# An orthogonal convolution by per-frequency solves: half 1's stores beside forming, the tables' products beside half 1's transform, two copies on ScalarE

## What is computed

```python
xfft = rfft2(pad(gn(x), 1), norm='ortho')            # 34 x 18 frequencies, 128 x 32 each
vfft = transpose(rfft2(weight, s=(34, 34)))          # 128 x 127 per frequency
vH   = conj(swapaxes(vfft, -1, -2))
wfft = vH @ vfft
wfft = wfft + eps[..., None, None] * eye(127)        # eps: mean diagonal * 1e-5
W    = I - 2.0 * (vfft @ solve(wfft, vH))            # 128 x 128 per frequency
z    = irfft2(W @ xfft)[..., 1:-1, 1:-1] + bias
out  = x + z
```

## Time and profile before

| | us |
|---|---|
| profiled execution | 3139.8 |
| its span, first to last instruction | 3137.1 |
| TensorE busy | 2606.8 (83%) |
| VectorE busy | 2014.0 (64%) |
| ScalarE busy | 1269.0 (40%) |
| GpSimd busy | 742.2 (24%) |
| mean granted clock of TensorE | 0.869 |

### The profile page before, as it was taken

How to read it: one execution, slowest core, us unless ns; L and a number is a source line. 1 busy time by engine, 2 the same in 40 slices (tenths; PEclk the granted TensorE clock), 3 DMA queues, 4 the chain that set the end, 5 groups by cost and what they waited for, 6 DMA issues and landing times. The chain is left out here.

```text
span 3137.1 us, 89161 instructions
## 1 busy us (share of the span) xinstructions
PE 2606.8 (83%) x38281; PEld 2133.8 (68%) x38281; DVE 2014.0 (64%) x3842; ACT 1269.0 (40%) x2963; POOL 742.2 (24%) x1307
## 2 busy tenths in 40 slices
PE   3994919889999888998886968778888879959999
PEld 3663915555666677877775747566676768859999
DVE  5453710779788787787778889697887782003333
ACT  0441402443534255555533534343454444632221
POOL 0340000312121042332431414031343242520000
PEclk7897969989999899999988989797988899976787
DMA  4348073314231064754733516060231232566662
GB/s 171 104 110 149 2 121 67 123 56 163 68 113 40 15 129 81 139 110 80 158 67 62 109 29 135 3 136 13 93 95 53 65 120 77 164 140 162 169 168 92
DMA packets 562599, 310.00 MB, mean 99 GB/s; under 512 B 484616, under 2 KB 495496, under 8 KB 561368
## 3 DMA queue, kind: packets, MB, share of 16 engines
q1 hardware_dynamic: 520896, 183.58, 28.5%
q0 software_dynamic: 41312, 120.73, 11.4%
HBM read 162.85 MB, written 141.30 MB: 97 GB/s over the span
## 5 line engine op out<-in xcount | busy, mean ns | idle before, releaser
L1386 DVE SCALAR_TENSOR_TENSOR arena<-arena,psum 128x512 f32<-128x512 f32 (+2 forms) x608 | 399.0, 719 | 280.2 <-PE psum L1016 279.9
L1349 DVE TENSOR_TENSOR arena<-arena 128x960 f32<-128x960 f32 (+24 forms) x480 | 420.2, 876 | 16.6
L1344 DVE TENSOR_TENSOR arena<-arena 128x960 f32<-128x960 f32 (+8 forms) x600 | 403.9, 723 | 8.3
L953 PE MATMUL psum<-arena 128*32 128x256 f32 (+1 forms) x2904 | 263.9, 430 | 90.9 <-DMA arena<-plain 73.9
L995 PEld LDWEIGHTS psum<-arena 32*32 32x32 f32 x9280 | 160.5, 118 | 256.9 <-issue 240.4
L871 POOL COPY arena<-arena 128x512 f32<-128x512 f32 (+2 forms) x160 | 87.1, 594 | 1040.0 <-ACT arena L1159 1040.0
L1016 PE MATMUL psum<-arena 32*128 32x64 f32 x9280 | 313.1, 282 | 9.8 <-ACT arena L1180 9.8
L1016 PEld LDWEIGHTS psum<-arena 32*128 32x128 f32 x9280 | 291.7, 197 | 34.5 <-ACT arena L1180 20.4
L995 PE MATMUL psum<-arena 32*32 32x64 f32 x9280 | 187.0, 235 | 135.9 <-DVEq L1378 125.7
L957 PE MATMUL psum<-arena 128*32 128x256 f32 (+1 forms) x3696 | 264.5, 373 | 0.0
L1159 ACT COPY arena<-arena 32x128 f32<-32x128 f32 (+3 forms) x496 | 222.2, 448 | 31.4 <-DVE arena L1386 12.5
(11 more groups left out here) (121 smaller groups left out, 4764.9 us busy)
## 6 DMA issues: line engine op xcount, KB each, us to landing
blocks<-arena POOLq DMA_DIRECT2D x145, 256.0 KB, 2.5
arena<-blocks SPq DMA_DIRECT2D x290, 128.0 KB, 2.8
kept<-arena POOLq DMA_DIRECT2D x145, 256.0 KB, 3.0
arena<-kept SPq DMA_DIRECT2D x145, 256.0 KB, 2.8
xhat<-arena SPq DMA_DIRECT2D x32, 580.0 KB, 13.0
arena<-xhat SPq DMA_DIRECT2D x580, 32.0 KB, 2.6
yhat<-arena POOLq DMA_DIRECT2D x290, 64.0 KB, 2.3
arena<-x SPq DMA_DIRECT2D x8, 2048.0 KB, 11.7
```

What stands on the lines that cost most here:

```text
L953: pe.matmul(columns[quadrant(p)].rearrange("p (a k) n -> p a k n", k=m), K["ident"][:, quadrant(p)], spread(base[:, 0:m, :], 1, n), start= ...
L1344: ins = dve.tensor_tensor(pr, spread(R[:, t, :, :, j], 3, 2 * w_), both, ALU.mult)
L1349: link(dve.tensor_tensor(rest, rest, pr[:, :, h], op))
L1386: ins = dve.scalar_tensor_tensor(old, old, K["mask"][:, piv:piv + 1], upd_bank(u, c)[:, 0:L * n].rearrange("p (t n) -> p t n", n=L), ALU.m ...
```

## The change

- `statistics` of half 0 moves in front of VectorE's wait for the correlations in stage one. The two instructions that form `eps_all` move to stage two, behind the normalization of the second sample.
- The 48 term products, their copies and with them their stores go between the parts of half 1 instead of half 0. SyncE loads row blocks 0 and 1 at the start of stage two as before, and blocks 2 to 7 behind the 16 stores of half 0; its loads of half 1's x have no row loads between them any more.
- The 16 stores of half 1 leave stage two. SyncE issues them in the solver, behind the first two table loads of form a. The first users of the memory that `xs` shares wait for them: `load_tables` of the first pre job, ScalarE's first copy to `staged`, VectorE's first `place`. For this, group a's part of `M` and group b's change places (`HOME`), and `ce`, the factors, moves below `M`.
- `copy_p` and `copy_q` move from GpSimd to ScalarE. In mid, ScalarE does `copy_p(m + 1)` right behind `copy_j(m + 1)`; in final, `copy_q(m)` right behind `copy_jq(m)`. GpSimd keeps the stores and the resets. ScalarE now waits at the start of a mid and of a final job for the updates of the sweeps before.

```diff
@@ -35,7 +35,7 @@
 SLOTS_OF = [FIRST[n + 1] - FIRST[n] for n in range(5)]
 GROUPS = [(0, 1, 2), (3, 4)]
 NT = max(len(sets) for sets in GROUPS)
-HOME = [0, 82]
+HOME = [NQ - 82, 0]
 RESIDENT = NQ
 NTERM = 5
 UNITS_OF_SET = [[8] * 4, [8] * 4, [6] * 3, [8] * 4, [8, 8, 8, 7]]
...
@@ -259,7 +259,14 @@
         mv = forward(HALF, 2)
         FORWARD_TOP = forward.at
         s_x = [ctx.enter_context(nc.semaphore(f"s_x{i}")) for i in range(4)]
-        s_mv = ctx.enter_context(nc.semaphore("s_mv"))
+        s_mv, s_eps, s_stored = (ctx.enter_context(nc.semaphore(n)) for n in ("s_mv", "s_eps", "s_stored"))
+
+        def store_half(sp, h):
+            for p in range(NP):
+                for r in range(2):
+                    lo = 2 * B * (p % LB) + B * r
+                    sp.dma_start(xhat[p // LB, h, lo:lo + B, :], xs[p * B:p * B + B, r, :, :].rearrange(
+                        "i f b -> i (f b)")).then_inc(s_stored, 16)
 
         def load_x(sp, h, q):
             sp.dma_start(x_half[:, 4 * q:4 * q + 4, :],
...
@@ -359,6 +366,7 @@
                         dve.wait_ge(s_chain, n[0])
 
                     ident_d = spread(K["ident"], 1, ND)
+                    statistics(dve, 0, link, 0)
                     dve.wait_ge(s_const, 32)
                     dve.wait_ge(s_a_copied, nbank)
                     link(dve.tensor_tensor(diag, shift_sb, ident_d, ALU.mult))
...
@@ -367,10 +375,6 @@
                     link(dve.tensor_copy(e_d, psum[3][:, 0:ND]))
                     link(dve.tensor_tensor(diag, ident_d, spread(e_d, 2, C), ALU.mult))
                     dve.tensor_tensor(shift_sb, shift_sb, diag, ALU.add).then_inc(s_shift, 1)
-                    statistics(dve, 0, link, 0)
-                    dve.wait_ge(s_tab, 16)
-                    link(dve.tensor_tensor(eps_prod, eps_tab, spread(e_d, 1, NQ), ALU.mult))
-                    dve.tensor_reduce(eps_all, eps_prod, AX.X, ALU.add)
             nc.all_engine_barrier()
 
         a = forward
...
@@ -418,19 +422,12 @@
                     load_rows(0)
                     load_rows(1)
                     for q in range(4):
-                        for p in ((2,), (3,), (4, 5), (6, 7))[q]:
-                            load_rows(p)
                         sp.wait_ge(s_ta, 2 * (4 * q + 4))
                         load_x(sp, 1, q)
-                    for h in range(2):
-
-                        sp.wait_ge(s_s2_cp, 3 * (h + 1) * HALF)
-                        for p in range(NP):
-                            for r in range(2):
-                                lo = 2 * B * (p % LB) + B * r
-                                sp.dma_start(xhat[p // LB, h, lo:lo + B, :], xs[p * B:p * B + B, r, :, :].rearrange(
-                                    "i f b -> i (f b)")).then_inc(s_stored, 16)
-                    sp.wait_ge(s_stored, 16 * NP * 2 * 2)
+                    sp.wait_ge(s_s2_cp, 3 * HALF)
+                    store_half(sp, 0)
+                    for p in range(2, NP):
+                        load_rows(p)
 
                 @block.gpsimd
                 def _(pool):
...
@@ -486,7 +483,7 @@
                                 if 0 <= b - 1 < HALF:
                                     copy_1(h * HALF + b - 1, j)
                                 u = 3 * (b - 1) + j
-                                if h == 0 and 0 <= u < len(T_UNITS):
+                                if h == 1 and 0 <= u < len(T_UNITS):
                                     copy_term(u)
 
                 @block.tensor
...
@@ -633,6 +630,10 @@
                             c = h * HALF + b
                             if b + 1 < HALF:
                                 norm(c + 1)
+                            if c == 0:
+                                dve.wait_ge(s_eps, 16)
+                                link(dve.tensor_tensor(eps_prod, eps_tab, spread(e_d, 1, NQ), ALU.mult))
+                                link(dve.tensor_reduce(eps_all, eps_prod, AX.X, ALU.add))
                             if h == 0 and b >= AHEAD:
                                 sums(dve, 1, b - AHEAD)
                             for j in range(3):
...
@@ -644,8 +645,13 @@
 
 
 
+
         a = Carve(BASE_SOLVE)
+        NCE = NT
+        ce = a(NCE, SP_, 2 * B)
+        M_AT = a.at
         M = a(RESIDENT, QUAD, L)
+        assert BASE + 2 * NFREQ * HALF <= M_AT + HOME[0] * QUAD * L
         R = a(NT, B, 2, B)
 
         PROD_W = 4 * (B - 1) * B * NT
...
@@ -678,14 +682,14 @@
         table = lambda c: (c(KG, LB * L), c(KG, L))
         tiles = [table(early) for _ in range(2)]
         assert early.at <= a.at
-        early = Carve(BASE_SOLVE + HOME[1] * QUAD * L)
+        early = Carve(M_AT + HOME[1] * QUAD * L)
         tiles += [table(early) for _ in range(4)]
         staged = early(NST, QUAD, 2 * L)
         q_emb = emb.rearrange("p a b f q r m -> p (a b) f q r m")
         z_and_q = carve(work, 0, 2, QUAD, 2 * L)
         x_turned = carve(work, 4 * QUAD * L, 4, QUAD, NB)
 
-        tail_in = Carve(BASE_SOLVE)(NTAIL, QUAD, 2 * L)
+        tail_in = Carve(M_AT + HOME[0] * QUAD * L)(NTAIL, QUAD, 2 * L)
         ys = carve(work, 6 * QUAD * L, 2, 2, C)
         SOLVER_END = a.at
 
...
@@ -842,9 +846,13 @@
 
                     for at, (kind, g, k, lo, hi) in enumerate(jobs):
                         if kind in ("form", "pre"):
+                            if kind == "pre" and k == 0:
+                                sp.wait_ge(s_stored, 16 * NP * 2 * 2)
                             for n, (of, _, first, _, _, _) in enumerate(loads):
                                 if of == kind and lo <= first < hi:
                                     load_tables(n)
+                                if n == 1 and at == 0:
+                                    store_half(sp, 1)
                         elif kind == "mid":
                             sp.wait_ge(S["formed"], before("form", at))
                             sp.wait_ge(S["pre_done"], NQ)
...
@@ -925,19 +917,10 @@
                                 for n in range(2):
                                     pool.wait_ge(S[f"y_stored{n}"], 32 * len(final_quads[n:before("final", at):2]))
                             for m in range(lo, hi):
-                                copy_p(m)
-                                if m > lo:
-                                    store_part(m - 1)
-                            store_part(hi - 1)
+                                store_part(m)
                         elif kind == "final":
-                            pool.wait_ge(S["s_done"], before("mid", at))
-                            pool.wait_ge(S["upd_copied"], 2 * before("sweep", at))
-                            for m in range(lo, min(lo + 4, hi)):
-                                copy_q(m)
                             for m in range(lo, hi):
                                 store_y(m)
-                                if m + 4 < hi:
-                                    copy_q(m + 4)
                     for n in range(2):
                         pool.wait_ge(S[f"y_stored{n}"], 32 * len(final_quads[n::2]))
                         pool.wait_ge(S[f"part_stored{n}"], 16 * len([q for q in mid_quads if q % 2 == n]))
...
@@ -1187,6 +1170,19 @@
                         act.copy(staged[:, m % NST].rearrange("p f (b n) -> p b f n", b=2),
                                  psum[6 + m % 2].rearrange("p (b f n) -> p b f n", b=2, f=QUAD)).then_inc(S["pre_copied"], 1)
 
+                    def copy_p(m):
+                        if m >= 2:
+                            act.wait_ge(S["s_done"], m - 1)
+                        src = M[:, home(mid_quads[m]), :, :]
+                        dst = emb[:, m % 2, 1].rearrange("p f q r m -> p (f q) r m")[:, :, 0, :]
+                        act.copy(dst, src.rearrange("p f n -> p (f n)").rearrange("p (a b) -> p a b", b=B))
+                        act.copy(work[:, m % 2, :, 0:L], src).then_inc(S["p_copied"], 1)
+
+                    def copy_q(m):
+                        src = M[:, home(final_quads[m]), :, :].rearrange("p f n -> p (f n)").rearrange("p (a b) -> p a b", b=B)
+                        dst = q_emb[:, m % 4].rearrange("p f q r m -> p (f q) r m")[:, :, 0, :]
+                        act.copy(dst, src).then_inc(S["q_copied"], 1)
+
                     def copy_b(m):
                         act.wait_ge(S[f"bx_in{m % 3}"], 48 * (m // 3 + 1))
                         if m >= 2:
...
@@ -1251,6 +1247,7 @@
                             for u in range(lo, hi):
                                 copy_form(u)
                         elif kind == "pre":
+                            act.wait_ge(s_stored, 16 * NP * 2 * 2)
                             for m in range(lo, hi):
                                 copy_blocks(m)
                         elif kind == "pivot":
...
@@ -1277,13 +1274,15 @@
                                 for n in range(2):
                                     act.wait_ge(S[f"y_stored{n}"], 32 * len(final_quads[n:before("final", at):2]))
```

(10 more changed lines are left out.)

27 lines of the change are left out of this document (6 added, 21 removed).

## The result

The kernel before took 3142.0 us in this comparison (median of 4 runs, 3126 to 3153), the changed one **3011.4 us** (median of 4, 3004 to 3034): ratio 0.960, 95% interval 0.953 to 0.967. The forecast was 3012. The profiled execution of the changed kernel took 3003.7 us (span 3001.9, granted clock 0.888), that of before 3139.8 (3137.1, 0.869).

| stretch (read from TensorE's timeline; a row ends where the next begins) | before | after | change | forecast |
|---|---|---|---|---|
| stage one, to the fourier load | 75.6 | 57.6 | -18.0 | -19 |
| stage two, to TensorE's last product | 328.4 | 317.9 | -10.5 | +5 |
| from there to the first forming product | 73.9 | 11.2 | -62.7 | |
| forming to mid a (stores beside it) | 625.8 | 626.1 | +0.3 | -59 with the row above |
| mid a with sweeps b | 503.9 | 500.1 | -3.8 | -15 |

What follows compares the result with a forecast made beforehand. No single bound: VectorE's chain in stage one, TensorE's order and uncovered stores in stage two, factors or a TensorE-ScalarE loop in the solver. -19 + 5 - 59 - 29 - 11 - 15 = -128 from 3139.8: 3012 us, range 2970 to 3060.

Steps and rivals of the forecast that it cites:

- Half 1's stores: Between stage two and forming: the 65.2 us of uncovered stores go, a late third table load costs 5; -59 us.
- Mid b: Mid of group b: without GpSimd's copies VectorE's four factors take 91.1 us each, all on the path; -29 us.
- VectorE ... just full; I take 0.5 us for 11 samples: Stage two, half 0: VectorE's work plus the next half's statistics just fills 5.91 us per sample; costs 5 us.
- I charge nothing: Stage two, half 0: transposes and transform products alone hold the high clock, so losing the term products costs nothing.
- The DMA term: Stage two: row block 0's table stores share the engines with half 0's stores, up to 9.5 us later; 7 taken.
- the free products: Stage two, half 1: eight term products issued before the stall become free, 8 x 1.19 = 9.5 us.
- The third rival: Stage two: half 0 stays at the low clock, as transposes don't count as activity; 80 us, 3092 us total; 3%.
- Forming's late table: Forming: the third table load, behind 16 stores on SP, makes unit 34 wait 5 us.
- Mid a: Mid of group a: ScalarE's two copies fit its 1.24 us idle, late solves and store waits shrink; -15 us.
- Final a: Final of group a: half of 8.0 us relief on each of four factors, capped by TensorE's 11.0 us wait; -11 us.
- The ends of all terms: Whole kernel: all terms' good and poor ends added up, given as 2964 and 3100 us.
- the first rival: Mid and final: ScalarE's copies end behind the schur product, up to 2.10 us lost per quad; 3329 us; 4%.

Runs made afterwards that it cites:

- two experiments: Changed kernel with copies p and q back on GpSimd: 3063.3 us; changed kernel with four unawaited GpSimd copies per quad added in mid b: 3033.3 us.
- The two experiments on it: Changed kernel with stores to kept on SP's queue: 3065.9 us; kernel with table-store wait and shift_mats edits, one mid load moved to GpSimd: 2998.0 us.

## Why the prediction was right, and where it was wrong

**Right in mechanism and size.** Stage one (-18.0 for -19): the statistics ended at 34.9, the chain at 49.7, the store took its 7.1 us. Half 1's stores (-62.7 + 0.3 for -59): the experiment that puts them back gives 63.0; 3.9 us of the sweeps' clock stand against the pauses in this sum. Mid b (-27.2 for -29): the factors fell to the 91 us that pre had shown, 27.5 us in sum, TensorE's parts and waits by 27.5, the sweeps by nothing. GpSimd's copies are the cause, by two experiments, and eleven kernels repeat the size within 1.5 us.

**Stage two (-10.5 for +5).** The step "VectorE ... just full; I take 0.5 us for 11 samples" failed: normalizations stayed 5.92 us apart with the next half's statistics between, and VectorE was busy 5.2 us of each (83.68 / 95.3 x 5.92). And "I charge nothing" for the clock was one-sided: the trace had 24 us at the low level with products in half 0, and the forecast read that as a proof that products don't help, not that they may delay the rise. Without them the clock rose 9.6 us in, worth 7.7 us. The DMA term (7) was measured at 8.4, and the free products (9.5) at 7.6. The kernel with the products back in half 0 is still 3.6 us shorter in this stage than the one before, and most of that is luck: in the kernel before the granted clock was 0.50 from 203.6 to 210.4 us, behind a TensorE pause of 2.1 us, and two normalizations lay 14.9 us apart. The kernel with the products back has a like pause, keeps the full clock, and has 11.8 us there. So some 3 of the 10.5 us are not the change's. The third rival fell: half 0, half of whose products are transposes, ran at a granted 1.00 from 71.5 on.

**Forming's late table.** The sum had 5 us for a third table load behind 16 stores. In the changed kernel's profile no unit waited for it, in five of the eleven made from it with these stores one did, up to 3.4 us; two pauses of 2.1 us came instead, which the forecast had no view of. The size was right by chance.

**Mid a (-3.8 for -15).** The -15 leaned on ScalarE's idle sums, 18.1 of late solves and 9.1 of kept waits, as if most of them would go. Half of the first went, and the second grew by 6.5: with the solves in time, copy t reaches the store of two quads before sooner than it lands (3.1 us behind an issue of 0.71), so the gain turned into the next wait. The two experiments on it: on SP the wait goes and the loads are late, with one load fewer on SP it falls to 4.7 and mid a gains 7 us (by what way wasn't looked for).

**Final a (-16.7 for -11): luck.** The four factors fell by 14.5 us in sum, near the 16 that the half relief gives, and TensorE's waits for them by 8.5, within the cap of 11.0. But the parts grew by 5.5, so the term itself came to -3.0 in this pair of profiles and to -7 by the means, and the other 13.7 us are the sweeps' clock.

**Two sums.** The ends of all terms give 3094 at the poor end and not 3100, or 3121 with the 27 us of final b. That the median lies within 1 us of the forecast is luck as well: errors of 15 and 11 us met, one kernel's runs spread over 30 us, and without the sweeps' 17 us the two profiles differ by 118 us, where 128 were forecast.

**ScalarE as the bound** (the first rival) never came near: its two copies of 0.41 us fit, and it still waits 0.81 us per quad of mid a for the schur product (66.2 / 82).

## What to carry to other kernels

When a wait is taken away, price the next one before the gain is booked: here the late solve hid a store two quads old, and behind that a queue that issued without a gap. Read the DMA queues' issue times like an engine's: six issues of 0.6 us fill a stretch of 3.6 us that is bound by TensorE and ScalarE, and a seventh makes the queue the bound. And before a term of 5 to 10 us is judged by total times, look at what the clock does in the same code of several profiles; here stretches tell and totals don't.
